# A decoder of two layers on one core: skip diagonals built first, and cross attention's first keys and queries prepared in another order

## The chip, the cores and the metric

The kernel runs on 1 core of one Trainium2 chip. The metric is the device time of one execution in microseconds. Before the change it is 2091.84 us, the median of 3 runs (2086.91 to 2093.14). A part of the program that its engines enter and leave together is called a block here; a barrier of all engines stands between two blocks.

## The reference, cut to what matters

The program computes two decoder layers on x (16 batches, 112 positions, 256 channels) with a context of 16 x 375 x 256. Each sublayer adds to x what it computes from the layer norm of x. The change touches the end of the first sublayer (a selective state space model) and the second (cross attention with 16 heads):

```
for the scan:      y_t = einsum('bdn,bn->bd', h, C_t);  y = y + xc * D;  out = (y * silu(z)) @ W_out + residual
cross attention:   q = x @ Wq + bq;   k, v = split(context @ Wkv + bkv)
                   q = _larope(q, Lq);   k = _larope(k, Lk)
                   scores = einsum('bhqd,bhkd->bhqk', q, k) * 64 ** -0.5
                   attn = softmax(where(context_mask, scores, -inf));   out = (attn @ v) @ Wo + bo
_larope:           re = te * cos - to * sin;   ro = te * sin + to * cos
```

The rest (routed experts, a gated recurrence, an attention by delays, a mixture with soft slots) is the same in both kernels.

## The kernel before

Tokens are columns, channels are partitions. The 1792 tokens are NCH = 4 chunks of CW = 448 columns, each of which holds BPC = 4 batches of L = 112. Every engine has its own instruction list, written out by hand in Python, and semaphores order them. An fp32 matmul of the program shows as two records in the trace.

The scan (`mamba`, lines 811 to 1060). The state space model runs in four passes of STEPS = 16 steps. A step is two scans and a product on VectorE (L988, L992, L997), two products on GpSimd (`feed_y` L932, `read_x` L938), exponentials and scalings on ScalarE (L884, L890, L895), and transposes and sums on TensorE (`feed_x` L1020, `add_up` L1025). Before the first step TensorE turns u (`turn_u`, L1013), VectorE copies it out of PSUM (`move_u`, L965), ScalarE scales it (L895), and TensorE turns the result into x_in (`feed_x(0, 0)`). The term xc * D comes in as a matmul with a diagonal matrix (L1045); VectorE builds its four diagonals (L978) after its four copies, and TensorE waits for them (skip_ready) ahead of `feed_x(0, 0)`.

The projection's block (`project_and_norm`, L1065 to 1152). TensorE projects the four chunks (L1086), VectorE adds them to x (L1120), ScalarE squares (L415), TensorE, ScalarE and VectorE make 1 / standard deviation of every column (L423, L428, L432), TensorE spreads it (L438) and VectorE multiplies (L444). SyncE loads cross attention's weights and the context of batches 0 and 1 in this block (`CrossWeights.load`). GpSimd has no work in it.

Cross attention's block (`cross_attention`). Scores are one bf16 matmul for each head, over 128 rows that hold the products of three bf16 parts of q and k. So q and k are split in three: ScalarE rounds the fp32 value to bf16 (`cast_queries` L1644, `cast_keys` L1606), GpSimd subtracts the rounded part (`lessen_queries` L1363, `lessen_keys` L1359), and ScalarE rounds the rest, until there are three parts. SyncE stores the parts to DRAM (L1309, L1303) and loads them back with a head's channels on the rows of the matmul (`load_queries` L1318, `load_keys` L1329). Before the split, keys and queries are turned (larope): TensorE projects them to PSUM (`keys` L1387, `queries` L1470), VectorE multiplies with cosines and sines out of PSUM (L1506, L1557), and the two halves are summed by GpSimd for keys (L1353, L1354) and by VectorE for queries (L1560, L1561).

At the block's start the order is: the centring of w_o and bo (`centre_columns`, L388 to L392, L1567), then for batches 0 and 1 the keys of that batch and the queries of chunk 0 and chunk 1, then the queries of chunks 2 and 3, then the values of batch 0 (L1398, L1596). SyncE stores and loads in the order keys' parts, queries' parts, keys, queries. Then `batch(b, s)` runs 16 times; in it head h is one turn of a software pipeline: score (L1408), mask and minimum on VectorE (L1518), exponential on ScalarE (L1615), transposes (L1418), copies (L1524, L1621), and the product with v every fourth head (L1433). Keys of batch b + 2 and values of batch b + 1 are made between the heads of batch b. The queries of chunks 2 and 3 are split by ScalarE and GpSimd between the heads of batch 0 at these places:

```
            CAST_QUERIES_AT = (0, 1, 3, 4, 6, 7)
            Q_CASTS = [[1, 2, 3], [4, 5, 6], [7, 9, 11], [8, 10, 12]]
```

## Time and profile before

| | us |
|---|---|
| median of 3 runs | 2091.84 |
| the profiled execution's own time | 2081.57 |
| its span, first to last instruction | 2079.8 |
| scan: its block starts, projection's block starts | 117.7, 469.2 |
| cross attention's block starts (first instruction of GpSimd) | 506.67 |
| first score of batch 0 starts | 542.70 |
| first exponential of batch 0 starts | 544.01 |

| engine | busy us | share of the span |
|---|---|---|
| TensorE | 1794.9 | 86% |
| VectorE | 1483.7 | 71% |
| ScalarE | 1051.8 | 51% |
| GpSimd | 901.1 | 43% |

The shares are over stages with different limits, so they say little of one place. A stage is read in the timeline, where a bracket behind an instruction gives how long its engine had been idle and what ended that.

### The profile page before, as it was taken

Reading aid. Unit: us, or ns where it says so; the run is one execution under the profiler, and the core shown is the slowest. Engines: PE = TensorE matmul, PEld = TensorE weight load, DVE = VectorE, ACT = ScalarE, POOL = GpSimd, SP = SyncE. Lnnn points to the kernel's source line nnn. Section 1 sums busy time; section 2 is a strip of 40 time slices with the busy share of each in tenths; the row PEclk is TensorE's granted clock in tenths of the full one; section 3 lists DMA queues with packets and bytes.
Section 4 is the critical chain, followed back from the end, with each engine's and each line's share of the span. In section 5 each row is a group of like instructions: output and inputs, shape, how many; then the busy total and the mean of one; then the engine's idle time right before and its main releaser. Section 6 shows DMA issues by size and latency. Waiting matters only on the chain. (4 is left out here: it accounts for less than half of the span.)

```text
span 2079.8 us, 32873 instructions
## 1 busy us (share of the span) xinstructions
PE 1794.9 (86%) x11062; PEld 1111.9 (53%) x11062; DVE 1483.7 (71%) x2738; ACT 1051.8 (51%) x2211; POOL 901.1 (43%) x602
## 2 busy tenths in 40 slices
PE   7958877879699999888788889888699989999799
PEld 4334444444476666544344444444564656665699
DVE  6779999994788888669555566555475448787893
ACT  4766666651677878526445455555332131114442
POOL 1269778771522222000466666666100009664342
PEclk9979999999899999999889999999899999999899
DMA  2034434331866566130355455543850044333640
GB/s 70 3 117 133 133 121 141 116 92 63 182 153 163 141 149 145 51 129 1 120 179 179 151 188 166 183 128 78 268 160 1 1 125 143 121 132 128 240 138 17
DMA packets 138157, 257.41 MB, mean 124 GB/s; under 512 B 30662, under 2 KB 94823, under 8 KB 135319
## 3 DMA queue, kind: packets, MB, share of 16 engines
q1 hardware_dynamic: 120358, 212.16, 34.2%
q0 software_dynamic: 13824, 37.77, 6.0%
q10 hardware_dynamic: 3808, 5.38, 1.1%
q8 instruction: 90, 1.47, 0.3%
q14 instruction: 77, 0.62, 0.1%
HBM read 205.82 MB, written 49.44 MB: 123 GB/s over the span
## 5 line engine op out<-in xcount | busy, mean ns | idle before, releaser
L3009 PE MATMUL moe_up_ps<-moe_w_tile,ahead 128*64 128x352 f32 x1152 | 213.7, 518 | 3.1 <-issue 1.1
L2946 POOL DMA_INDIRECT moe_y<-ahead,moe_where x144 | 161.9, 1125 | 120.2 <-DVE ahead L3079 91.1
L2940 POOL DMA_INDIRECT ahead<-moe_tok,moe_where x144 | 143.6, 997 | 147.6 <-POOLq L2517 104.0
L2182 POOL TENSOR_TENSOR soft_power<-soft_logit,soft_high 128x1024 f32<-128x1024 f32 x28 | 66.2, 2366 | 292.8 <-DVE soft_high L2244 292.4
L3153 ACT ACTIVATE moe_w_tile<-moe_w 128x1216 f32 x144 | 175.5, 1220 | 19.7 <-issue 19.7
L1615 ACT ACTIVATE xattn_prob<-xattn_sm,xattn_least 112x375 f32<-112x375 f32 x256 | 154.9, 606 | 55.9 <-DVE xattn_least L1518 51.0
L1518 DVE CUSTOM_DVE_ANT_0 xattn_sm<-xattn_s_ps,xattn_mask 112x375 f32<-112x375 f32 x256 | 137.9, 544 | 51.6 <-PE xattn_s_ps L1408 30.2
L938 POOL TENSOR_TENSOR mamba_x_state<-mamba_x_state,mamba_cx_all 128x896 f32<-128x896 f32 x64 | 133.8, 2090 | 69.1 <-DVE mamba_x_state L988 69.0
L1418 PE MATMUL xattn_pt_ps<-ident,xattn_prob 112*125 112x112 f32 x768 | 131.0, 280 | 20.6 <-ACT xattn_pt L1621 12.4
L1418 PEld LDWEIGHTS xattn_pt_ps<-ident,xattn_prob 112*125 112x125 f32 x768 | 112.3, 189 | 60.6 <-ACT xattn_prob L1615 43.7
L3009 PEld LDWEIGHTS moe_up_ps<-moe_w_tile,ahead 128*64 128x64 f32 x1152 | 85.4, 152 | 102.6 <-issue 93.8
L932 POOL TENSOR_TENSOR xn<-mamba_u,mamba_b_all 128x896 f32<-128x896 f32 x64 | 133.8, 2093 | 13.2 <-DMA mamba_b_all<-mamba_b 13.0
L988 DVE TENSOR_TENSOR_SCAN mamba_x_state<-xn,mamba_x_in 128x896 f32<-128x896 f32 x64 | 128.6, 2010 | 1.9 <-PE mamba_x_in L1020 1.9
L992 DVE TENSOR_TENSOR_SCAN mamba_y_state<-mamba_y_state,xn 128x896 f32<-128x896 f32 x64 | 128.4, 2006 | 0.4 <-ACT mamba_y_state L890 0.4
L3073 DVE TENSOR_TENSOR moe_hid<-ahead,moe_up_ps 128x176 f32<-128x176 f32 x144 | 45.7, 333 | 106.0 <-ACT ahead L3159 67.9
L895 ACT ACTIVATE mamba_scaled<-mamba_w_in,mamba_b_turned 128x256 f32<-128x256 f32 x224 | 96.0, 497 | 44.6 <-PE mamba_x_in L1020 43.6
L1020 PE MATMUL mamba_x_in<-ident,mamba_scaled 128*128 128x128 f32 x448 | 63.3, 283 | 62.7 <-ACT mamba_scaled L895 40.3
L2930 DVE COPY moe_w_tile<-moe_w 128x1216 f32 x144 | 109.6, 803 | 10.0 <-issue 9.8
L1025 PE MATMUL mamba_y<-mamba_x_state,ident 128*128 128x448 f32 x256 | 107.6, 543 | 5.3 <-POOL mamba_x_state L938 5.2
L2273 ACT ACTIVATE soft_power<-soft_power 128x1024 f32<-128x1024 f32 x28 | 29.7, 1059 | 155.5 <-POOL soft_power L2182 155.5
L1025 PE MATMUL mamba_y<-ahead_small,ident 128*128 128x448 f32 x256 | 107.6, 543 | 0.0
L1020 PEld LDWEIGHTS mamba_x_in<-ident,mamba_scaled 128*128 128x128 f32 x448 | 49.7, 144 | 105.4 <-ACT mamba_scaled L895 60.5
(435 smaller groups left out, 4301.2 us busy)
## 6 DMA issues: line engine op xcount, KB each, us to landing
moe_w<-moe_w SPq DMA_DIRECT2D x64, 480.0 KB
soft_w<-soft_w SPq DMA_DIRECT2D x16, 1024.0 KB
mamba_b_all<-mamba_b SPq DMA_DIRECT2D x32, 448.0 KB, 4.6
mamba_cx_all<-mamba_c SPq DMA_DIRECT2D x32, 448.0 KB, 3.9
mamba_cy_all<-mamba_c SPq DMA_DIRECT2D x32, 448.0 KB, 4.6
moe_w_tile<-moe_y SPq DMA_DIRECT2D x14, 1024.0 KB, 7.8
soft_logits<-soft_logit SPq DMA_DIRECT2D x28, 512.0 KB
soft_logit<-soft_logits SPq DMA_DIRECT2D x14, 1024.0 KB, 5.4
```

Source lines behind the costliest of these rows:

```text
L932: pool.tensor_tensor(y_in[:, j % 2], u[:, c0 + j % 2, tok], b_all[:, n % 2], ALU.mult).then_inc(y_fed, 1)
L938: pool.tensor_tensor(x_state[:, j % 2], x_state[:, j % 2], cx_all[:, n % 2], ALU.mult).then_inc(x_read, 1)
L988: dve.tensor_tensor_scan(x_state[:, j % 2], x_decay[:, j % 2], x_in[:, 0:HW], 0.0, ALU.mult, ALU.add).then_inc(x_scanned, 1)
L992: dve.tensor_tensor_scan(y_state[:, 0:HW], y_state[:, 0:HW], y_in[:, j % 2], 0.0, ALU.mult, ALU.add).then_inc(y_scanned, 1)
L1025: mm = pe.matmul(y[:, j % 2, w, 0:CW], g.ident[:], src[:, j % 2, w * CW:(w + 1) * CW], start=False, stop=False, skip_group_check=True)
L1418: mm = pe.transpose(turned_probs(h)[:, c], prob[:, h % RING, c * KC:(c + 1) * KC], g.ident[0:L, 0:L])
L1518: dve.tensor_tensor_reduce(sm[:, h % RING], s_ps[0:L, h % 2, 0:S2], mask[:, s], -SCALE, BIG, ALU.add, ALU.min, least[:, s, head(h):head(h) ...
L1615: act.activation(prob[:, h % RING], sm[:, h % RING], ACT.Exp, bias=least[:, s, head(h):head(h) + 1], scale=-1.0, accum_out=total[:, s, hea ...
L2940: pool.indirect_dma_start(xg[:, 2 * s + i], None, tok_dram, bass.IndirectOffsetOnAxis(ap=where[:, 0, t:t + 1], axis=0)).then_inc(gathered[ ...
L2946: pool.indirect_dma_start(y_dram, bass.IndirectOffsetOnAxis(ap=where[:, 1, t:t + 1], axis=0), y_sb[:, 2 * s + i], None).then_inc(y_stored[ ...
L3009: mm = pe.matmul(up_ps[n * HALF:(n + 1) * HALF, i, 0:2 * I], xT[:, s % 2, at:at + HALF], w_tile[:, s, i, n, h * 2 * I:(h + 1) * 2 * I], st ...
L3153: place_weights = weight_placer(act, 0, lambda to, src: act.activation(to, src, ACT.Copy))
```

## The change

1. In the scan's block VectorE builds the four diagonals ahead of its four copies, and TensorE waits for them after `feed_x(0, 0)`, ahead of the first matmul that reads them.
2. The keys of batch 0 are projected, turned, split, stored and loaded in the projection's block, by a new class FirstKeys: two pairs of matmuls into a PSUM bank that before held every second chunk's spread factors, four products on VectorE, two sums and two subtractions on GpSimd, three casts on ScalarE, three stores and four loads on SyncE. The centring of w_o moves there too. The spread factors of chunks 0, 1 and 2 now share one bank, and chunk 3's go to a bank of the accumulator.
3. In cross attention's block the queries fall in five groups: batch 0 (112 columns), batches 1 to 3 (336 columns), and chunks 1, 2 and 3. Batch 0's are first on TensorE and VectorE; VectorE itself subtracts its parts; one store and its three loads are SyncE's first. Groups 0 and 1 are turned by VectorE as before. Of groups 2 to 4 ScalarE takes the projection out of PSUM with its bias (`keep_queries`, two of 128x448 each), and GpSimd turns them (`turn_queries`, four products and two sums of 128x448 each) while batches 0, 1 and 2 run; their three casts stand at heads 7, 11 and 14 of those batches and their stores behind the keys of batch b + 2. VectorE no longer turns those three chunks.
4. The tensors of the scan that reach into cross attention, and merged, q, q_turn and mask, lie in one tensor ("wide"), so the names in the new program differ. The two loads of the context are no longer next to each other: batch 1's is last in the list.

The diff, cut to its core:

```
         self.own_rows, self.w_kv, self.w_o = view(r, 1494, [NHEAD, D]), view(r, 1750, [P, DH, 2 * D]), view(r, 2774, [P, DH, D])
         self.context, self.keep = view(r, 3286, [P, 2, DH, S2]), view(r, 4786, [L, B * S2 // 4]).bitcast(U8)
         self.small_loaded, self.kv_loaded, self.w_o_loaded = k.kept_sem("xattn_small_loaded"), k.kept_sem("xattn_kv_loaded"), k.kept_sem("xattn_w_o_loaded")
+        self.rope_loaded = k.kept_sem("xattn_rope_loaded")
         self.ctx_loaded = [k.kept_sem(f"xattn_ctx_loaded{s}") for s in range(2)]
...
     def load(self, sp, ins):
         sp.dma_start(self.w_kv, ins["xattn_w_kv"].rearrange("(h p) n -> p h n", p=P)).then_inc(self.kv_loaded, 16)
-        for s in range(2):
-            self.load_context(sp, ins, s, s)
-        sp.dma_start(self.bias, ins["xattn_bias"]).then_inc(self.small_loaded, 16)
-        sp.dma_start(self.rope, ins["xattn_rope"]).then_inc(self.small_loaded, 16)
+        self.load_context(sp, ins, 0, 0)
+        sp.dma_start(self.bias, ins["xattn_bias"]).then_inc(self.rope_loaded, 16)
+        sp.dma_start(self.rope, ins["xattn_rope"]).then_inc(self.rope_loaded, 16)
+        sp.dma_start(self.w_o, ins["xattn_w_o"].rearrange("(c p) n -> p c n", p=P)).then_inc(self.w_o_loaded, 16)
         sp.dma_start(self.w_q, ins["xattn_w_q"].rearrange("(h p) n -> p h n", p=P)).then_inc(self.small_loaded, 16)
-        sp.dma_start(self.w_o, ins["xattn_w_o"].rearrange("(c p) n -> p c n", p=P)).then_inc(self.w_o_loaded, 16)
         sp.dma_start(self.own_rows, ins["xattn_own_rows"]).then_inc(self.small_loaded, 16)
-        sp.dma_start(self.keep, ins["xattn_keep"].partition_broadcast(L)).then_inc(self.kv_loaded, 16)
+        sp.dma_start(self.keep, ins["xattn_keep"].partition_broadcast(L)).then_inc(self.small_loaded, 16)
+        self.load_context(sp, ins, 1, 1)
...
+class FirstKeys:
...
+    def project(self, pe, m, to):
+        c = self.g.cross
+        if m == 0:
+            pe.wait_ge(c.kv_loaded, 16)
+            pe.wait_ge(c.ctx_loaded[0], 16)
+        else:
+            pe.wait_ge(self.half_read, 1)
+        for h in range(DH):
+            mm = pe.matmul(to[:, 0:S2], c.w_kv[:, h, m * P:(m + 1) * P], c.context[:, 0, h], start=(h == 0), stop=(h == DH - 1))
+        mm.then_inc(self.ready, 1)
+
...
+        dve.wait_ge(self.ready, m + 1)
+        cos, sin = c.rope[:, 2 * L:2 * L + S2], c.rope[:, 2 * L + S2:]
+        for n in range(2):
+            product = dve.scalar_tensor_tensor(self.turn[:, 2 * m + n], src[:, 0:S2], c.bias[:, DH + m:DH + m + 1], (cos, sin)[(m + n) % 2], ALU.add, ALU.mult)
+        product.then_inc(self.read if m else self.half_read, 1)
+
+    def centre_out(self, dve):
+        dve.wait_ge(self.g.cross.w_o_loaded, 16)
+        centre_columns(dve, Steps(dve, self.w_o_centred), self.g.cross.w_o, self.w_o_total, self.w_o_mean[:])
+
+    def split(self, act, n):
+        if n == 0:
+            act.wait_ge(self.whole, 1)
+        else:
+            act.wait_ge(self.less, n)
+        act.activation(self.part[:, n], self.key[:], ACT.Copy).then_inc(self.cast, 1)
...
+        pool.wait_ge(self.half_read, 1)
+        pool.wait_ge(self.read, 1)
+        pool.tensor_tensor(key[:, 0], turn[:, 0], turn[:, 2], ALU.subtract)
+        pool.tensor_tensor(key[:, 1], turn[:, 1], turn[:, 3], ALU.add).then_inc(self.whole, 1)
+        for n in range(self.PARTS - 1):
+            pool.wait_ge(self.cast, n + 1)
+            pool.tensor_tensor(key[:], key[:], self.part[:, n], ALU.subtract).then_inc(self.less, 1)
+
+    def move(self, sp):
+        for n in range(self.PARTS):
+            sp.wait_ge(self.cast, n + 1)
+            sp.dma_start(self.dram[0, DH * n:DH * (n + 1)].rearrange("m p t -> p m t"), self.part[:, n]).then_inc(self.stored[n], 16)
+        for first, last, at in sorted(self.K_ROWS, key=lambda rows: rows[1]):
+            sp.wait_ge(self.stored[last - 1], 16)
+            rows = (last - first) * HD
+            sp.dma_start(self.ks[at:at + rows, 0], self.dram[0, DH * first:DH * last].rearrange("n (i h) t -> (n i) h t", h=NHEAD)).then_inc(self.loaded[0], 16)
 
...
-                    for r in range(TURNED):
-                        move_u(0, r)
                     for c in range(DIC):
                         diag = dve.tensor_scalar(skip_diag[:, c], g.ident[:], skip[:, c:c + 1], None, ALU.mult)
                     diag.then_inc(skip_ready, 1)
+                    for r in range(TURNED):
+                        move_u(0, r)
...
-                    pe.wait_ge(skip_ready, 1)
                     for p, (c0, hh) in enumerate(passes):
                         feed_x(p, 0)
+                        if p == 0:
+                            pe.wait_ge(skip_ready, 1)
...
+        places, after = [spread[:, s] for s in range(2)], None
+        if keys:
+
+            places, after = [spread[:, 0]] * 3 + [acc[:, 1, 0]], [0, 1, 2, 0]
+        ln = ChunkNorm(k, ctx, name, g, [var[:, i % 2, 0:L] for i in range(NCH)], places, after)
...
             project(0)
             project(1)
             ln.variance(pe, 0, 0)
+            if keys:
+                keys.project(pe, 0, raw_keys)
             project(2)
             ln.spread_out(pe, 0)
             ln.variance(pe, 1, 0)
+            if keys:
+                keys.project(pe, 1, raw_keys)
             project(3)
             ln.spread_out(pe, 1)
             ln.variance(pe, 2, 1)
@@ -1124,9 +1221,14 @@
             add(0)
             add(1)
             ln.invert(dve, 0)
+            if keys:
+                keys.rotate(dve, 0, raw_keys)
             add(2)
             ln.scale(dve, 0)
             ln.invert(dve, 1)
+            if keys:
+                keys.rotate(dve, 1, raw_keys)
+                keys.centre_out(dve)
             add(3)
             ln.scale(dve, 1)
             ln.invert(dve, 2)
@@ -1142,8 +1244,13 @@
             ln.root(act, 0)
             ln.square(act, 2, added, 3 * DH)
             ln.root(act, 1)
+            if keys:
+                keys.split(act, 0)
+                keys.split(act, 1)
             ln.square(act, 3, added, 4 * DH)
             ln.root(act, 2)
+            if keys:
+                keys.split(act, 2)
             ln.root(act, 3)
...
-            CAST_QUERIES_AT = (0, 1, 3, 4, 6, 7)
+            CAST_QUERIES_AT = (7, 11, 14)
...
+            FIRST, OTHERS = 0, 1
+            GROUPS = [(0, slice(0, L)), (0, slice(L, CW))] + [(j, slice(0, CW)) for j in range(1, NCH)]
+            Q_PLACES = (s_ps, pt_ps, s_ps, pt_ps, s_ps)
...
+                store_queries(FIRST)
+                sp.wait_ge(q_first_stored, 16)
+                load_queries(0, 0)
+                store_parts(1, 1)
+                load_keys(1, 1)
+                store_queries(OTHERS)
+                sp.wait_ge(q_stored[0], 16 * (BPC - 1))
+                load_queries(1, 1)
+                for b in range(B - 2):
+                    if b == 2:
...
+                    pool.tensor_tensor(query(g_no, 1), turned_query(g_no, 1), turned_query(g_no, 3), ALU.add).then_inc(q_whole, 1)
 
                 pool.memset(v[:], 0.0).then_inc(v_cleared, 1)
-                for s in range(2):
-                    sum_keys(s)
-                    for n in range(PARTS - 1):
-                        lessen_keys(s, n)
-                        lessen_queries(s, s, n)
+                sum_keys(1)
+                pool.wait_ge(q_whole, 2)
                 for n in range(PARTS - 1):
-                    for j in range(2, NCH):
-                        lessen_queries(j, j % 2, n)
+                    lessen_keys(1, n)
+                    lessen_queries(OTHERS, n)
                 for b in range(B - 2):
+                    if b < NCH - 1:
+                        turn_queries(OTHERS + 1 + b)
                     sum_keys(b + 2)
                     for n in range(PARTS - 1):
...
+                def keep_queries(g_no):
+
+                    act.wait_ge(q_ready, g_no + 1)
+                    for m in range(DH):
+                        last = act.activation(query(g_no, m), query_ps(g_no, m), ACT.Identity, bias=bq[:, m:m + 1])
+                    last.then_inc(q_kept, 1)
```

In the scan's block, VectorE's list from the end of its clearing to the first scan. Before:

```order
L960 MEMSET xn 128x8 x2
L965 COPY mamba_w_in<-mamba_x_in 128x512 x2
L965 COPY mamba_w_in<-mamba_y_state 128x512
L965 COPY mamba_w_in<-mamba_y_state 128x256
L978 TENSOR_SCALAR ahead_small<-ident,mamba_small 128x128 x4
L988 SCALAR_TENSOR_TENSOR mamba_x_state<-xn,mamba_x_in 128x896
```

With the change:

```order
L1041 MEMSET xn 128x8 x2
L1057 TENSOR_SCALAR ahead_small<-ident,mamba_small 128x128 x4
L1046 COPY wide<-mamba_x_in 128x512 x2
L1046 COPY wide<-mamba_y_state 128x512
L1046 COPY wide<-mamba_y_state 128x256
L1069 SCALAR_TENSOR_TENSOR mamba_x_state<-xn,mamba_x_in 128x896
```

The four diagonals (ahead_small is their place) moved ahead of the four copies; nothing else did.

At the start of cross attention's block, TensorE's list up to the first scores (s_ps, pt_ps and kv_ps are PSUM tensors that queries, keys and values are projected to). Before:

```order
L1476 MATMUL xattn_o_ps<-ahead,mean_w 128x1 x2
L1387 MATMUL xattn_kv_ps<-ahead 128x375 x4
L1470 MATMUL xattn_s_ps<-xn,ahead 128x448 x4
L1387 MATMUL xattn_kv_ps<-ahead 128x375 x4
L1470 MATMUL xattn_pt_ps<-xn,ahead 128x448 x4
L1470 MATMUL xattn_s_ps<-xn,ahead 128x448 x4
L1470 MATMUL xattn_pt_ps<-xn,ahead 128x448 x4
L1398 MATMUL xattn_kv_ps<-ahead 125x256 x6
```

With the change:

```order
L1626 MATMUL xattn_s_ps<-xn,ahead 128x112 x4
L1633 MATMUL xattn_o_ps<-ahead,mean_w 128x1 x2
L1537 MATMUL xattn_kv_ps<-ahead 128x375 x4
L1626 MATMUL xattn_pt_ps<-xn,ahead 128x336 x4
L1626 MATMUL xattn_s_ps<-xn,ahead 128x448 x4
L1548 MATMUL xattn_kv_ps<-ahead 125x256 x4
L1626 MATMUL xattn_pt_ps<-xn,ahead 128x448 x4
L1548 MATMUL xattn_kv_ps<-ahead 125x256 x2
L1626 MATMUL xattn_s_ps<-xn,ahead 128x448 x4
```

One set of key matmuls is gone, batch 0's queries are first, and the values stand between the chunks.

ScalarE's list at the same place, with the change, from the first cast of group 1's queries to the first exponentials (before, six casts of keys and six of queries alternate, then come the copies of the values, the table load and the exponentials):

```order
L1815 ACTIVATE xattn_q_part<-wide 128x2x336
L1756 ACTIVATE xattn_v<-xattn_kv_ps 125x8x16 x4
L1821 ACTIVATE wide<-xattn_pt_ps,ahead 128x448 x2
L1766 ACTIVATE xattn_part<-xattn_key 128x750
L1815 ACTIVATE xattn_q_part<-wide 128x2x336
L122 DMA ahead<-ctxT 128x2x375
L1756 ACTIVATE xattn_v<-xattn_kv_ps 125x8x16 x2
L1821 ACTIVATE wide<-xattn_s_ps,ahead 128x448 x2
L1766 ACTIVATE xattn_part<-xattn_key 128x750
L1815 ACTIVATE xattn_q_part<-wide 128x2x336
L1775 ACT_TABLE_LOAD
L1775 ACTIVATE xattn_prob,xattn_total<-xattn_sm,xattn_least 112x375 x6
```

Behind the last chunk's matmuls there now stand on ScalarE two of `keep_queries`, a cast of keys, a cast of queries and the table load, all ahead of the first exponential.

## Rows read from the trace of the kernel before

**Rows 1.** Timeline, start of the scan's block: start us, us, engine, what [idle, releaser].

```profile
119.95 2.89 ACT L895 ACTIVATE mamba_scaled<-mamba_w_in,mamba_b_turned 128x256 f32<-128x256 f32 x7
...
121.44 4.11 POOL L932 TENSOR_TENSOR xn<-mamba_u,mamba_b_all 128x896 f32<-128x896 f32 x2 [12.95 <-DMA mamba_b_all<-mamba_b]
121.52 4.51 DVE L978 TENSOR_SCALAR ahead_small<-ident,mamba_small 128x128 f32<-128x128 f32 x4
...
126.09 1.76 PE L1020 MATMUL mamba_x_in<-ident,mamba_scaled 128*128 128x128 f32 x7 [5.12 <-DVE ahead_small L978]
...
127.95 2.02 DVE L988 TENSOR_TENSOR_SCAN mamba_x_state<-xn,mamba_x_in 128x896 f32<-128x896 f32 x1 [1.92 <-PE mamba_x_in L1020]
```

**Rows 2.** Windows: us, busy PE, PEld, DVE, ACT, POOL (instructions), granted clock, DMA, GB/s.

```profile
469.20:504.90 35.70, 34.45 (x194) 18.54 (x194) 12.51 (x16) 6.91 (x11) 0.00 (x0) 1.00 0.26 85
506.60:542.70 36.10, 23.25 (x64) 12.99 (x65) 27.49 (x38) 12.87 (x19) 21.04 (x13) 0.81 0.45 103
542.70:563.20 20.50, 18.33 (x146) 12.83 (x146) 15.15 (x47) 16.91 (x43) 10.75 (x7) 0.84 1.02 205
563.20:582.60 19.40, 18.32 (x197) 13.66 (x185) 16.33 (x52) 15.55 (x48) 4.80 (x4) 1.00 0.75 176
```

**Rows 3.** Timeline, from cross attention's block start to its first exponential.

```profile
506.67 2.66 POOL L1365 MEMSET xattn_v<- 125x3072 f32 x1 [42.36 <-POOLq L78]
...
507.30 4.32 PE L1387 MATMUL xattn_kv_ps<-ahead 128*128 128x375 f32 x8
...
514.61 2.69 PE L1387 MATMUL xattn_kv_ps<-ahead 128*128 128x375 f32 x8
...
522.93 2.28 DVE L1560 TENSOR_TENSOR xattn_q<-xattn_q_turn 128x448 f32<-128x448 f32 x1
...
523.14 3.17 PE L1470 MATMUL xattn_pt_ps<-xn,ahead 128*128 128x448 f32 x8
526.15 1.89 PE L1398 MATMUL xattn_kv_ps<-ahead 128*125 128x256 f32 x8
...
540.00 1.28 ACT L1615 ACT_TABLE_LOAD   x1
...
542.70 0.85 PE L1408 MATMUL xattn_s_ps<-xattn_ks,xattn_qs 128*112 128x375 bf16 x2 [3.69 <-DMA xattn_qs<-xattn_q_parts]
...
544.01 0.61 ACT L1615 ACTIVATE xattn_prob<-xattn_sm,xattn_least 112x375 f32<-112x375 f32 x1 [2.73 <-DVE xattn_least L1518]
```

**Rows 4.** Groups by form, 506 to 543 us: busy us, mean ns, idle before.

```profile
L1363 POOL TENSOR_TENSOR xattn_q<-xattn_q,xattn_q_part 128x896 f32<-128x896 f32 x4 | 7.9, 1981 | 2.5 <-ACT xattn_q_part L1644 2.5
...
L1644 ACT ACTIVATE xattn_q_part<-xattn_q 128x896 bf16<-128x896 f32 x6 | 5.7, 949 | 7.8 <-POOL xattn_q L1363 4.7 <-DVE xattn_q L1561 3.1
L1606 ACT ACTIVATE xattn_part<-xattn_key 128x750 bf16<-128x750 f32 x6 | 5.0, 828 | 16.0 <-POOL xattn_key L1354 13.7 <-POOL xattn_key L1359 2.3
...
L1557 DVE SCALAR_TENSOR_TENSOR xattn_q_turn<-xattn_s_ps,ahead 128x448 f32<-128x448 f32 x8 | 4.9, 678 | 2.1 <-PE xattn_s_ps L1470 2.0
```

**Rows 5.** Timeline, two forms that come near to new ones.

```profile
488.06 1.04 PE L438 MATMUL mamba_proj_out_spread<-mamba_proj_out_ln_rstd,pick 128*128 128x112 f32 x8
...
886.76 0.63 ACT L1152 ACTIVATE mean<-xattn_proj_out_acc,xattn_bo_mean 128x448 f32<-128x448 f32 x1 [0.40 <-PE xattn_proj_out_acc L1093]
```

**Rows 6.** DMA issues, 566 to 580 us: count, KB each, median us to landing.

```profile
xattn_qs<-xattn_q_parts SPq DMA_DIRECT2D x2, 168.0 KB, 2.8
```

**Rows 7.** Timeline, batches 0 and 1.

```profile
553.22 3.74 POOL L1363 TENSOR_TENSOR xattn_q<-xattn_q,xattn_q_part 128x896 f32<-128x896 f32 x2 [0.47 <-ACT xattn_q_part L1644]
...
554.07 0.50 DVE L1524 COPY xattn_pt<-xattn_pt_ps 125x336 f32<-125x336 f32 x1
...
563.24 0.35 DVE L1512 TENSOR_SCALAR xattn_mask<-ahead 112x375 f32<-112x375 uint8 x1
...
565.14 0.61 ACT L1615 ACTIVATE xattn_prob<-xattn_sm,xattn_least 112x375 f32<-112x375 f32 x1 [0.47 <-DVE xattn_least L1518]
...
582.60 0.34 DVE L1512 TENSOR_SCALAR xattn_mask<-ahead 112x375 f32<-112x375 uint8 x1
```

307 lines of the change are left out of this document (194 added, 113 removed).

## The prediction

> **What bounds the kernel now.** I read the page's shares first, then the windows of the stages that the change touches [rows 2], then the timeline at three places [rows 1, 3, 5, 7] and the groups for durations [rows 4]. TensorE's 86% says little. In the projection's block it is the bound (34.45 of 35.7 us busy [rows 2]). In the first 36 us of cross attention it is busy for 23.25, at a mean granted clock of 0.81, and no engine is full: that stretch is a chain. It ends with batch 0's first score at 542.70, after TensorE waited 3.69 us for a load of queries, and the first exponential at 544.01 [rows 3]. Before that load stand the keys of batch 0, four query stores, four key loads and three query loads. In the scan VectorE runs one scan after another, so what delays its first delays all: TensorE sat idle 5.12 us until the last diagonal, and the scan began at 127.95 [rows 1].
>
> **1. Diagonals first: -3.2 us.** The diagonals ran from 121.52 for 4.51 us, beside GpSimd's two products (121.44 for 4.11), and `feed_x(0, 0)` began at 126.09. The other thing that it waits for, ScalarE's seven scalings, ends at 119.95 + 2.89 = 122.84 [rows 1]. With the diagonals at about 118, before GpSimd has work, it begins at 122.9, 3.2 us earlier, and the scan with it: 124.8. The copies of u may be later by the diagonals' own time; GpSimd's feeds (done at 125.55) are needed only at the second scan, 2 us later. Bounds: 0, if another input of the first step takes over; -3.3 at most.
>
> **2. Keys in the projection's block: +2.7 us.** TensorE gets four fp32 matmuls of 375 columns there, 2.69 us for that form at full clock [rows 3], and it is the bound [rows 2]. The rest lies beside it: VectorE's four products, the centring of w_o, GpSimd's four operations and ScalarE's three casts (0.83 each [rows 4]) fit in idle time (VectorE 12.51 and ScalarE 6.91 busy of 35.7, GpSimd 0 [rows 2]). What they could hold up is the last add and the last square. If that cover fails, the centring and a cast show: I allow 2.5 us more. SyncE's last key loads must be issued before the block ends; the third cast is about 6 us ahead of the end, a store lands in some 3 us (loads of like size took 2.8 [rows 6]). Bounds: +1.3 (half of the matmuls) and +5.2. The next block then starts at 506.67 - 3.2 + 2.7 = 506.2.
>
> **3. The start of cross attention: -12.2 us to the first exponential.** I add up TensorE from the block's start (506.67 before; its keys begin 0.6 later, behind the sums for bo [rows 3]). Batch 0's queries are eight records of 112 columns: 1.04 us for that form at full clock [rows 5], twice that at half clock, as the trace has it at this start (keys 4.32 us there against 2.69 later [rows 3]). So the keys of batch 1 start at 0.6 + 2.1 = 2.7. Those slow keys ended 5.0 us after the start; I take half of the present ones in that time (2.2) and half after it (1.4): 6.3. Group 1, three quarters of 3.17: 8.7. Chunk 1, 3.17: 11.9. Two thirds of the values, 1.89: 13.8. Chunk 2: 17.0. The last values 1.0: 18.0. Chunk 3: 21.1 [rows 3]. Then ScalarE: two `keep_queries` (0.63 each, by the nearest form [rows 5], overlapping a little) 1.2; only here are the scores let go, at 22.3. A cast of keys 0.83, a cast of three quarters of the queries' 0.95 [rows 4], and the table load of 1.28 [rows 3], which before lay in idle time and now stands in the way: first exponential 25.1 us after the start. Before it was 544.01 - 506.67 = 37.3. Difference -12.2.
>
> I put the DMA path below that. Batch 0's queries are projected by 2.9 and turned by 4.7 (a product of 448 columns takes 0.678 us [rows 4], here a quarter of the columns), cast and lessened in turn with VectorE's key products by about 10, stored (one store instead of four) by 13, and loaded by 17: loads of this kind landed in 2.8 us where the queues were free [rows 6]. So some 5 us of cover lie before 22.3. Batch 1's queries follow its keys and their stores and land at about 38 by the same prices; its first score is due at 22.3 + 21.1 = 43.4 (544.01 to 565.14 [rows 3, 7]). Bounds: -16 (table and last casts hidden, clock full from the start) and -8 (the queries' load last, 4 us late).
>
> **4. Batches 0 to 2: +1.0 us.** From first exponential to the next batch's mask batch 0 took 563.24 - 544.01 = 19.2 us, batch 1 582.60 - 565.14 = 17.5 [rows 7]. Batch 0 had six query casts and a mean clock of 0.84 [rows 2]; so six casts and a slow start cost 1.8 together, a cast at most 0.3. Now each of three batches has three casts: batch 0 loses three casts and the slow start (-0.9), batches 1 and 2 gain three each (+1.7). GpSimd's turning is six operations of 448 columns, about 1.0 us each by half of 1.98 [rows 4], 6 us a batch beside 3.9 of subtractions and 4.8 of keys [rows 2]: 15 of 19.4 us. VectorE's wait for GpSimd is the new cost. `TENSOR_TENSOR` with both inputs in SBUF took 2.28 us while GpSimd worked [rows 3], and the diagonals 4.51 [rows 1], but copies out of PSUM took 0.50 beside it [rows 7]. In a batch only the mask and one reciprocal of VectorE work from SBUF alone; I take +0.2. Here a rule bears. The Trainium skill ("SBUF — State Buffer", section "Who interferes with whom") says that such a pair excludes each other for a whole instruction, while a VectorE instruction with at most one SBUF input outside its two-port modes does not contend. By it the price is at most two waits of one GpSimd operation for each batch, and the rows above agree. Bounds: -2 and +5.
>
> **Sum:** -3.2 + 2.7 - 12.2 + 1.0 = -11.7 us. Against the profiled execution's own 2081.57 us (span 2079.8) that is 2069.9. The median of the runs shown is 2091.84, 0.5% above that execution; the same difference on it gives **2080.1 us**. A measurement of this kernel can tell about 0.3% (6.3 us) from no change.
>
> **The rivals.**
> - *The chain at the start gets shorter still.* TensorE keeps its full clock and ScalarE's last casts slip in before the keeps: part 3 gives -16 and batch 0 runs at batch 1's pace with its casts. Gain 3.2 - 2.7 + 16 + 0 = 16.5: 2075. For it: of those 25 us, 2.8 are casts and table load and more than 4 are at half clock. Against it: ScalarE's list is in order and the table load is behind the last cast.
> - *ScalarE becomes the bound of batches 1 and 2.* It is busy 15.55 of 19.4 us in batch 1 [rows 2]; three casts of 0.95 make 18.4. If every cast shows, part 4 is 6 x 0.95 - 0.9 + 0.2 = +5.0: gain 7.7, 2084.1. Against it: six casts in batch 0 cost 1.8 at most.
> - *The diagonals do nothing.* If another input of the first step (a load of b or c, a decay) comes as late, 3.2 is missing: 2083.3. Against it: the rows show none after 125.6.
> - *Slower: GpSimd keeps VectorE out.* If every operation of VectorE in batches 0 to 2, not only those from SBUF alone, waited for GpSimd, the added GpSimd work would go on top: 9.9 us in each, less batch 0's four subtractions of 1.98 [rows 4] that are gone, 22 in all. -3.2 + 2.7 - 12.2 + 22 = +9.3, 2101.1. It decides from about 13 us of such waits. For it: 2.28 us for a sum of 448 columns while GpSimd worked [rows 3]. Against it: 0.50 for the copy in the middle of GpSimd's work [rows 7].
>
> **How the numbers follow.** Forecast 0.62, shorter chain 0.12, ScalarE 0.14, diagonals 0.07, slower 0.05. The range reaches from the shorter chain's 2075 less 2 for the runs' own spread to the ScalarE case's 2084.1 with part 2 at its upper bound (+2.5) and the same spread: 2073 to 2089. Faster by over 0.3% means below 2085.6: the forecast nearly always (0.59), the first rival (0.12), the others that remain in half their cases (0.10): 0.81. Within 0.3%: 0.14. Slower: 0.05.
>
> **What the profile would show.** Right: first scan at about 124.8 with TensorE's wait for ScalarE, not the diagonals; cross attention's block starts at about 506.2; first score at about 528.5 with no DMA as releaser but ScalarE's keep; first exponential at about 531.3 behind a table load; mask to mask in batches 1 and 2 under 20.5 us. Wrong: the first score waiting for a load of queries or of keys; the projection's block longer by over 5 us, or ended by SyncE; batch 1's first score waiting for its queries; VectorE's operations out of PSUM longer than 0.5 us in batches 0 to 2.

## The result and the profile after

| | before | after |
|---|---|---|
| median of 18 runs, us | 2095.26 | 2083.31 |
| lowest and highest, us | 2086.91, 2099.80 | 2075.81, 2095.41 |
| span of the profiled execution, us | 2079.8 | 2074.0 |

The ratio is 0.9939, 95% interval 0.9928 to 0.995: 12.8 us less by the ratio, 10.5 to 15.1 by its interval. The forecast was 11.7 us less and 2080.1, with a range of 2073 to 2089.

First the scan, by the timeline (start us, us, engine, line, operation, in brackets the idle time before it and what ended that). It answers to [rows 1].

```profile
115.23 0.29 DVE L1057 TENSOR_SCALAR ahead_small<-ident,mamba_small 128x128 f32<-128x128 f32 x1
115.43 0.67 DVE L1057 TENSOR_SCALAR ahead_small<-ident,mamba_small 128x128 f32<-128x128 f32 x3
117.34 2.88 ACT L976 ACTIVATE mamba_scaled<-wide,mamba_b_turned 128x256 f32<-128x256 f32 x7
...
120.28 1.76 PE L1101 MATMUL mamba_x_in<-ident,mamba_scaled 128*128 128x128 f32 x7 [1.92 <-ACT mamba_scaled L976]
...
122.14 2.02 DVE L1069 TENSOR_TENSOR_SCAN mamba_x_state<-xn,mamba_x_in 128x896 f32<-128x896 f32 x1 [3.15 <-PE mamba_x_in L1101]
```

The four diagonals take under 1 us, where beside GpSimd they took 4.51, and TensorE now waits for ScalarE's scalings, as forecast. The block starts at 115.10 (117.72 before; what lies ahead is the same program, so these 2.6 us are the execution's own). From the block's start the scan begins after 7.04 us instead of 10.23.

Next the start of cross attention, against [rows 3]. The block starts at 503.18, and the distances behind the rows are from there.

```profile
503.18 2.66 POOL L1514 MEMSET xattn_v<- 125x3072 f32 x1 [8.95 <-POOLq L78]
503.37 2.02 PE L1626 MATMUL xattn_s_ps<-xn,ahead 128*128 128x112 f32 x8 [3.25 <-PEq L78]
...
505.93 4.48 PE L1537 MATMUL xattn_kv_ps<-ahead 128*128 128x375 f32 x8
...
510.24 2.42 PE L1626 MATMUL xattn_pt_ps<-xn,ahead 128*128 128x336 f32 x8
...
512.50 3.17 PE L1626 MATMUL xattn_s_ps<-xn,ahead 128*128 128x448 f32 x8
...
514.72 1.23 SPq L1452 DMA_DIRECT2D xattn_qs<-xattn_q_parts  x3
514.73 0.51 DVE L1715 TENSOR_TENSOR wide<-wide 128x336 f32<-128x336 f32 x1
...
521.11 3.17 PE L1626 MATMUL xattn_s_ps<-xn,ahead 128*128 128x448 f32 x8
...
524.31 1.16 ACT L1821 ACTIVATE wide<-xattn_s_ps,ahead 128x448 f32<-128x448 f32 x2 [1.01 <-PE xattn_s_ps L1626]
...
525.52 0.53 PE L1558 MATMUL xattn_s_ps<-xattn_ks,xattn_qs 128*112 128x375 bf16 x2 [1.25 <-ACT wide L1821]
...
526.86 1.28 ACT L1775 ACT_TABLE_LOAD   x1
...
528.15 0.61 ACT L1775 ACTIVATE xattn_prob<-xattn_sm,xattn_least 112x375 f32<-112x375 f32 x1
```

From the block's start, batch 1's keys begin after 2.75 us, group 1 after 7.06, chunk 1 after 9.32, the last chunk ends at 21.1, the first score runs at 22.34, released by ScalarE's keep (the copy of the last chunk's queries out of PSUM) and not by a load, and the first exponential at 24.97, right behind the table load. Before, it was 37.34. Batch 0's queries are loaded by 11.5 + 1.2 (three issues) + 2.9 (the median landing of such loads here) = 15.7, by estimate.

The windows (us, busy PE, PEld, DVE, ACT, POOL with counts, granted clock, DMA share, GB/s) of the projection's block, of the start, and of batches 0 to 3, which answer to [rows 2].

```profile
463.10:503.20 40.10, 36.98 (x202) 20.05 (x202) 16.85 (x23) 9.40 (x14) 4.79 (x5) 0.99 0.47 127
503.20:525.50 22.30, 20.90 (x64) 13.21 (x64) 7.84 (x21) 8.41 (x20) 10.51 (x8) 0.86 0.25 66
525.50:545.70 20.20, 17.39 (x146) 12.28 (x146) 14.88 (x47) 15.72 (x41) 11.51 (x10) 0.92 0.67 136
545.70:566.40 20.70, 18.62 (x194) 13.74 (x186) 16.26 (x52) 17.73 (x52) 15.10 (x12) 1.00 0.84 177
566.40:587.30 20.90, 18.38 (x190) 13.60 (x186) 16.31 (x52) 18.01 (x54) 15.11 (x12) 1.00 0.82 177
587.30:608.10 20.80, 18.29 (x189) 13.60 (x185) 16.38 (x53) 17.32 (x52) 6.62 (x5) 1.00 0.84 178
```

The projection's block is 40.1 us long instead of 37.5 (469.2 to 506.67). Its last cast of keys and the loads of them:

```profile
494.26 0.83 ACT L186 ACTIVATE xattn_part<-xattn_key 128x750 bf16<-128x750 f32 x1
495.52 3.74 SPq L205 DMA_DIRECT2D xattn_ks<-xattn_k_parts  x4
```

In the start TensorE is busy for 20.9 of 22.3 us. ScalarE is busy for 17.3 to 18.0 of 20.8 us in batches 1 to 3. From mask to mask these batches take 20.7, 20.9 and 20.7 us, where before they took 19.4, 20.1 and 20.1.

Where the sum of the two traces then goes is the surprise. At the last exponential the changed kernel is 14.7 us ahead (844.8 against 859.5), at the first product of the routed experts 17.2 (988.0 against 1005.2). The experts' stage, where the change does nothing, took 463.4 us instead of 450.6, and the end is 5.8 us ahead. Yet the medians say 12. The kernel before was profiled in an execution of 2081.57 us, below all of its 18 runs (the lowest is 2086.91); the changed one in its fastest (2075.81). So the two traces understate the change. The first question for the runs was still whether the change slows the experts.

### The profile page after: what moved, and what is told of

Same layout as the page of the kernel before. It is cut to its first block and busy times, and to the rows that moved or that the text cites. A ratio compares the mean times of both kernels' runs of the same rounds, so it can differ in the third digit from the quotient of the medians.

```text
span 2074.0 us, 32902 instructions
## 1 busy us (share of the span) xinstructions
PE 1790.3 (86%) x11070; PEld 1111.4 (54%) x11070; DVE 1463.1 (71%) x2728; ACT 1053.7 (51%) x2220; POOL 917.2 (44%) x620
## 5 line engine op out<-in xcount | busy, mean ns | idle before, releaser
L1676 DVE CUSTOM_DVE_ANT_0 xattn_sm<-xattn_s_ps,wide 112x375 f32<-112x375 f32 x256 | 137.6, 542 | 54.0 <-PE xattn_s_ps L1558 26.3
L1013 POOL TENSOR_TENSOR xn<-mamba_u,mamba_b_all 128x896 f32<-128x896 f32 x64 | 133.9, 2095 | 14.9 <-DMA mamba_b_all<-mamba_b 14.7
L3115 DVE COPY moe_w_tile<-moe_w 128x1216 f32 x144 | 109.2, 799 | 11.3 <-issue 11.0
L976 ACT ACTIVATE mamba_scaled<-wide,mamba_b_turned 128x256 f32<-128x256 f32 x224 | 95.8, 495 | 40.2 <-PE mamba_x_in L1101 39.2
L1682 DVE COPY xattn_pt<-xattn_pt_ps 125x336 f32<-125x336 f32 x192 | 96.5, 503 | 16.2 <-PE xattn_pt_ps L1568 15.7
```

The lines of the kernel that those rows point to most:

```text
L1013: pool.tensor_tensor(y_in[:, j % 2], u[:, c0 + j % 2, tok], b_all[:, n % 2], ALU.mult).then_inc(y_fed, 1)
L1676: dve.tensor_tensor_reduce(sm[:, h % RING], s_ps[0:L, h % 2, 0:S2], mask[:, s], -SCALE, BIG, ALU.add, ALU.min, least[:, s, head(h):head(h) ...
```

## The experiments

In every kernel below, each copy that places an expert's weights waits against the expert's number masked with 63 (one register operation more, in the experts' stage); `before_again` shows that it costs nothing visible (a ratio of 0.9999). Kernels of one group ran on one chip, and the three groups on three chips; for the first pair the record names no chip. A mask (the row of VectorE that makes one batch's mask) marks the same point of each batch; times from mask to mask are read from the timelines, and batch 1 runs from mask 1 to mask 2.

**The pair again, and the diagonals alone and undone.**

> The kernel before, with one register operation more at each of the copies that place an expert's weights (the number that the copy waits for is masked with 63); the base of the others. Theory: within 0.2% of the kernel before, stages as in its trace, and a routed-experts stage (first to last product of moe_up) that differs between profiles of one kernel by some +-6 us, near 455 in the mean. Rival (the change itself slows the experts by the 12.8 us that the two traces differ by): this kernel has 450 to 452 again, after_again 462 to 465.

> The changed kernel, with the same mask. Theory: 11 to 14 us less than before_again in the medians; experts' stage within 5 us of before_again's in the second pair of profiles, so that the 12.8 us of the first pair are the runs' own spread. Rival: the experts' stage is 10 us or more longer again, and then the difference up to the experts must be 22 us or more.

> before_again with the diagonals ahead of the copies of u and nothing else of the change. Theory: first scan 3.2 us earlier after its block's start (7.0 instead of 10.2), released by ScalarE's scalings; total -3 us. Rival (another input or a later wait of the scan takes it back): first scan earlier but the projection's block starts at the same distance from the scan's block as in before_again, total 0 within 1 us.

```diff
-                    for r in range(TURNED):
-                        move_u(0, r)
                     for c in range(DIC):
...
                     diag.then_inc(skip_ready, 1)
+                    for r in range(TURNED):
+                        move_u(0, r)
...
-                    pe.wait_ge(skip_ready, 1)
                     for p, (c0, hh) in enumerate(passes):
                         feed_x(p, 0)
+                        if p == 0:
+                            pe.wait_ge(skip_ready, 1)
```

> after_again with the diagonals back behind the copies of u. Theory: +3.2 us against after_again, first scan 10.2 us after its block's start; cross attention as in after_again, so the rest of the change alone is worth 9 us. Rival (parts depend on each other or the diagonals are hidden): no difference within 1 us.

Its edit is the same one backwards. Measured on one chip, the kernel before at 2022.45 us (35 runs):

| kernel | median us | ratio to before | interval | scan begins | experts' stage |
|---|---|---|---|---|---|
| before_again | 2022.43 | 0.9999 | 0.998 to 1.0017 | 125.9 | 391.3 |
| before_diag | 2021.65 | 0.9995 | 0.9975 to 1.0016 | 122.6 | 390.7 |
| after_nodiag | 2012.75 | 0.9956 | 0.9935 to 0.9977 | 125.9 | 392.9 |
| after_again | 2012.02 | 0.9949 | 0.9931 to 0.9968 | 122.2 | 394.1 |

The change is worth 10.3 us here (6.5 to 14.0 by the interval), a little under the 11 to 14 expected. The experts' stage does not lengthen by 12.8 us again; it is 2.8 longer in this pair and 2.2 in the other, so the rival (10 us or more) is gone, though 2 to 3 us are not excluded. On this chip the stage is 60 us shorter than the 455 us that I expected, in all four kernels; the last section takes that up. The diagonals' move is plain in the rows, `before_diag` first, `before_again` behind it:

```profile
120.71 1.76 PE L1020 MATMUL mamba_x_in<-ident,mamba_scaled 128*128 128x128 f32 x7 [1.92 <-ACT mamba_scaled L895]
122.57 2.02 DVE L988 TENSOR_TENSOR_SCAN mamba_x_state<-xn,mamba_x_in 128x896 f32<-128x896 f32 x1 [3.15 <-PE mamba_x_in L1020]
```

```profile
119.47 4.54 DVE L978 TENSOR_SCALAR ahead_small<-ident,mamba_small 128x128 f32<-128x128 f32 x4
124.06 1.75 PE L1020 MATMUL mamba_x_in<-ident,mamba_scaled 128*128 128x128 f32 x7 [5.15 <-DVE ahead_small L978]
125.92 2.02 DVE L988 TENSOR_TENSOR_SCAN mamba_x_state<-xn,mamba_x_in 128x896 f32<-128x896 f32 x1 [1.92 <-PE mamba_x_in L1020]
```

From ScalarE's scalings (117.77 and 117.90) the scan begins 4.80 us later instead of 8.02, so it gains 3.2; in the other pair it is 4.80 and 8.01. Counted from the start of the scan's block, the projection's block begins 3.7 us earlier (348.4 against 352.1), and 3.9 in the other pair (348.2 against 352.1), so no later wait of the scan takes it back. But the totals differ by 0.8 and 0.7 us where 3 were expected, and each has an interval of some 4 us to either side. A gain of 3 us is shown at its place, and neither shown nor refuted in the time.

**The start made shorter, in three steps.** The kernel before: 2080.84 us (27 runs).

> after_again with one exponential of a single element put on ScalarE before the last keeps of queries, so that the exponentials' table is loaded there, where ScalarE waits for TensorE. Theory (the start is a chain of TensorE's list and then ScalarE's list in its order): the load of 1.28 us goes off the path, first exponential 1.3 us earlier after the block's start (23.7 instead of 25.0), first score unchanged at 22.3. Rival (the batch 0 loads or the first score's bias set it): under 0.3 us. Total -1 us, less than the medians can tell.

```diff
                 copy_values(0, 0, 2)
+                act.activation(recip[0:1, 0:1], g.ident[0:1, 0:1], ACT.Exp)
                 keep_queries(4)
```

> table, and the last cast of batch 1's keys and of its queries put behind the first three exponentials. Theory: the first exponential then waits only for the first score, its bias of 0.55 us and the table: score 22.3 + 0.2 + 0.6 = 23.1 after the block's start; the 1.5 us of casts come back behind it only in part, batch 1's keys and queries being ready with 5 us to spare. Rival (batch 1's loads become late): TensorE waits for a load at batch 1's first score and the mask-to-mask time of batch 0 rises by over 1 us.

```diff
-                cast_keys(1, 2)
-                cast_queries(OTHERS, 2)
                 for h in range(3):
                     exponentiate(0, 0, h)
+                cast_keys(1, 2)
+                cast_queries(OTHERS, 2)
```

> table_casts, and the first three scores put ahead of the last chunk's queries on TensorE, those queries written where the sums of the first batches come (free until the first weigh), with their keeps on ScalarE behind the first exponentials. Theory: batch 0's queries and keys are in place by 17 us after the block's start, so the first score runs at about 18.2 (after the last values) and the first exponential at about 19.2, 5.8 us earlier than in after_again; the 3.2 us of queries and 1.2 us of keeps then stand in batch 0, where TensorE is near its bound, so that mask 1 comes only 2 to 4 us earlier. Total -2 to -4 us against after_again. Rival (the path of batch 0's queries over DMA is the real bound and has no cover): the first score waits for a load of queries or keys, and the gain at the first exponential is under 2 us.

```diff
-            Q_PLACES = (s_ps, pt_ps, s_ps, pt_ps, s_ps)
+            Q_PLACES = (s_ps, pt_ps, s_ps, pt_ps, o_ps)
...
+                pe.wait_ge(q_kept, 1)
+                for h in range(3):
+                    scores(0, 0, h)
                 queries(4)
-                pe.wait_ge(q_kept, 3)
-                for h in range(4):
-                    scores(0, 0, h)
+                scores(0, 0, 3)
+                pe.wait_ge(q_kept, 2)
                 for h in range(2):
                     turn_probs(0, 0, h)
+                pe.wait_ge(q_kept, 3)
...
+                for h in range(3):
+                    exponentiate(0, 0, h)
                 keep_queries(4)
-                for h in range(3):
-                    exponentiate(0, 0, h)
                 cast_keys(1, 2)
```

Distances from the block's start in us:

| kernel | ratio to before (interval) | first score | first exponential | mask 1 | batch 1 | batch 2 | batch 3 |
|---|---|---|---|---|---|---|---|
| before, first trace | | 36.0 | 37.3 | 56.6 | 19.4 | 20.1 | 20.1 |
| after, first trace | 0.9939 (0.9928 to 0.995) | 22.3 | 25.0 | 42.5 | 20.7 | 20.9 | 20.7 |
| table | 0.996 (0.9935 to 0.9985) | 22.7 | 23.9 | 40.0 | 20.7 | 20.9 | 22.4 |
| table_casts | 0.9967 (0.9952 to 0.9981) | 22.6 | 23.7 | 40.6 | 23.7 | 22.5 | 20.7 |
| early_scores | 0.9967 (0.9955 to 0.9979) | 17.9 | 21.5 | 39.4 | 24.6 | 20.9 | 22.4 |

`table` gains 1.0 us at the first exponential, not 1.3, since the table load and its one-element exponential held the last keep up by 0.5 us (it starts at 526.09, TensorE's last chunk ends at 525.64). But at mask 1 it gains 2.5, and the rest has another cause. Windows of the changed kernel, then of `table`, around and behind the first exponential (the last three numbers are the granted clock, DMA share, GB/s):

```profile
526.00:529.00 3.00, 0.88 (x4) 0.35 (x3) 1.58 (x6) 2.97 (x6) 3.00 (x4) 1.00 0.65 144
529.00:532.00 3.00, 2.99 (x12) 2.14 (x13) 2.27 (x7) 2.27 (x8) 2.90 (x3) 0.64 0.99 188
532.00:535.00 3.00, 3.00 (x14) 2.18 (x13) 1.44 (x4) 1.20 (x5) 0.00 (x0) 0.79 1.02 240
```

```profile
526.00:529.00 3.00, 0.99 (x4) 0.41 (x4) 1.04 (x5) 3.00 (x7) 3.00 (x4) 1.00 0.03 10
529.00:532.00 3.00, 2.99 (x17) 2.03 (x18) 2.70 (x9) 2.27 (x9) 2.92 (x3) 1.00 1.03 225
532.00:535.00 3.00, 3.00 (x38) 2.12 (x37) 2.65 (x9) 2.23 (x7) 1.36 (x2) 1.00 0.99 196
```

In the changed kernel TensorE has only four scores to do between 524.3 and 528.9, and behind that stretch its clock is at 0.64 and 0.79 of 2.4 GHz, a mix of the two levels; in 529 to 535 it gets 26 matmuls of its list through. In `table` the stretch is 3.6 us (525.6 to 529.2), the clock stays at 1.00, and 55 of the same list get through. All seven profiles with the table load in its old place show the lower clock there (0.60 to 0.68 and 0.76 to 0.83 in the two windows of 3 us behind the stretch), and the three with only the table load and casts moved (`table`, `table_casts`, `best`) show 1.00. That the clock makes all of the other 1.5 us is not measured by itself.

`table_casts` and `early_scores` show the other wall. In `early_scores` the first score runs at 17.9 with no wait for a load, so batch 0's loads have at least the 4.4 us of cover down to 22.3. Its first exponential was expected at 19.2 and came at 21.5: the table load stands behind two casts and a copy of values on ScalarE, and the exponential comes right behind it. Its rows of the first score, of the table load, and of batch 1's first score:

```profile
522.43 0.48 PE L1558 MATMUL xattn_s_ps<-xattn_ks,xattn_qs 128*112 128x375 bf16 x2
524.64 1.28 ACT L1855 ACT_TABLE_LOAD   x1
546.56 0.34 PE L1558 MATMUL xattn_s_ps<-xattn_ks,xattn_qs 128*112 128x375 bf16 x1 [1.86 <-issue]
```

Batch 1 has less cover. The loads of its queries and its first score, in `table_casts`:

```profile
545.42 2.65 SPq L1452 DMA_DIRECT2D xattn_qs<-xattn_q_parts  x6
...
549.68 0.53 PE L1558 MATMUL xattn_s_ps<-xattn_ks,xattn_qs 128*112 128x375 bf16 x1 [2.24 <-issue]
```

In the changed kernel, by the timeline of SyncE's queue and of TensorE:

```profile
530.56 1.90 SPq L1443 DMA_DIRECT2D xattn_q_parts<-xattn_q_part  x3
539.42 6.53 SPq L1452 DMA_DIRECT2D xattn_qs<-xattn_q_parts  x6
...
546.36 0.32 PE L1558 MATMUL xattn_s_ps<-xattn_ks,xattn_qs 128*112 128x375 bf16 x1
```

There they are in by 539.42 + 1.2 (three issues) + 2.9 = 543.5, by estimate, 2.8 us ahead of use. From the last issue of the stores ahead of them (532.46) to the first load it is 7.0 us, and batch 1's key loads stand in front of these stores; that they are the cause was not separated. Two casts behind three exponentials moved the first load from 36.2 to 39.3 us after the block's start, and TensorE waited 2.24 us, with the clock at 0.50 for the 3 us behind it. The profile names no releaser ("issue"), but the same estimate puts the queries in at 545.42 + 1.2 + 2.9 = 549.5, and the score starts at 549.68. What `early_scores` won at the start it paid in batch 1, 24.6 us. So the rival named for `table_casts` came true (batch 1's loads are late; the time shows in batch 1, not in batch 0). The one named for `early_scores` did not: batch 0's path has cover, and it is batch 1's that has none to spare. (The single batches of 22.4 and 22.5 us are taken up in the last section.)

None of the three ratios (0.996 to 0.9967) is better than the changed kernel's (0.9939, and 0.9949 on another chip), and those of `table_casts` and `early_scores` have intervals above its first one. The changed kernel did not run on this chip, so this is no direct comparison. The rows agree with it: `table_casts` gains 2.0 us to mask 1 and loses 4.6 in batches 1 to 3, `early_scores` gains 3.1 and loses 5.5; `table` gains 2.5 and loses 1.6, all of it in batch 3.

**What lengthens batches 1 to 3.** The next kernel was executed once, on the same chip.

> after_again without ScalarE's nine casts of queries in batches 0 to 2 (what is stored for batches 4 to 15 is then the parts of the first chunk; the output leaves the other chunks' queries out). It tells what lengthens batches 1 to 3 by 0.7 to 1.4 us against before. If it is ScalarE: mask to mask in batches 1, 2 back to 19.4 to 20.1. If it is GpSimd's turning (VectorE kept out, or keys late): 20.7 and 20.9 stay, within 0.2.

```diff
-                        if b < NCH - 1 and h in CAST_QUERIES_AT:
-                            cast_queries(OTHERS + 1 + b, CAST_QUERIES_AT.index(h))
```

Beside these lines, the stores and GpSimd's subtractions of these groups no longer wait for a cast; GpSimd does the same work, 15.1 us in each of batches 1 and 2.

Batches 1 to 3 took 20.3, 19.9 and 19.6 us, 2.6 in sum less than in the changed kernel, and batch 0 did not move (mask 1 at 42.5). So in sum ScalarE's casts, with what waits for them, make 2.6 of the 2.8 us by which these batches had grown, and GpSimd's turning next to nothing (the three batches take 59.8 us without the casts, and 59.5 to 59.8 in the three profiles with the old cross attention). Batch by batch it is less clean: the casts cost 0.45, 1.06 and 1.1 us, and batch 1 stays 0.9 us above the 19.4 of the kernel before, while batches 2 and 3 are 0.3 and 0.4 below its 20.1. The cause of that stays open. Batch 3 has only one cast, the one at head 14 of batch 2, and it cost 1.1 us. The trace shows how: it stands ahead of ScalarE's copy of turned probabilities, and TensorE waits for that copy. Three such waits stand in the changed kernel's timeline, and in the same batches TensorE has no wait over 1 us in `no_casts`, in `before` or in `casts_moved` below:

```profile
550.92 0.55 PE L1568 MATMUL xattn_pt_ps<-ident,xattn_prob 112*125 112x112 f32 x3 [1.45 <-ACT xattn_pt L1781]
571.81 0.55 PE L1568 MATMUL xattn_pt_ps<-ident,xattn_prob 112*125 112x112 f32 x3 [1.44 <-ACT xattn_pt L1781]
592.73 0.55 PE L1568 MATMUL xattn_pt_ps<-ident,xattn_prob 112*125 112x112 f32 x3 [1.44 <-ACT xattn_pt L1781]
```

**The casts moved, the best start, and GpSimd's work doubled.** The kernel before: 2093.49 us (11 runs).

> after_again once more, on the chip of the next three: their base. Theory: 0.5 to 0.6% under the kernel before; mask-to-mask times of the first batches as in both traces of it (20.7, 20.9, 20.7) and a granted clock below 1.00 for some 6 us behind the first exponential.

> after_third with ScalarE's first cast of each group of queries at head 5 instead of 7, and its last at head 4 of the next batch instead of head 14. In the trace ScalarE runs without a gap from head 7 of a batch to head 2 of the next, and idles before heads 1 to 6. Theory (a cast costs its full 0.9 us where ScalarE has no gap, nothing where it has): mask to mask 20.2 in batch 1, 19.9 in batch 2, 19.7 in batch 3, 2 us less in all. Rival (the casts cost by what they trigger: GpSimd's subtractions beside VectorE): the three stay above 20.6.

```diff
-            CAST_QUERIES_AT = (7, 11, 14)
+            CAST_QUERIES_AT = (5, 11)
...
+                        if 0 < b < NCH and h == 4:
+                            cast_queries(OTHERS + b, 2)
```

> casts_moved, with the exponentials' table loaded by a one-element exponential at the very start of ScalarE's list, where it is idle for 5 us. Theory: first score 22.3 and first exponential 23.6 us after the block's start (25.0 in after_third); the stretch in which TensorE does little shortens from 4.6 us to 3.2 and its clock stays at 1.00 behind it, worth 1.5 us more; with the casts, 5 us less than after_third. Rival (the compiler puts a second table load where it was): no difference from casts_moved.

```diff
+                act.activation(recip[0:1, 0:1], g.ident[0:1, 0:1], ACT.Exp)
                 for n in range(PARTS):
                     cast_first(n)
```

> after_third with GpSimd's four products of each turned group done twice (the same result; 4.4 us more of GpSimd in each of batches 0 to 2). Theory: GpSimd has gaps of 3.4 us and more before the keys' sums, VectorE's operations read at most one operand from SBUF: up to 1 us more per batch, by keys that become whole later. Rival (GpSimd keeps VectorE out, the slower case of the prediction): 4.4 us more per batch, the copies out of PSUM longer than 0.5 us.

```diff
+                    for time in range(2):
-                    for n, table in enumerate((q_cos, q_sin, q_sin, q_cos)):
+                        for n, table in enumerate((q_cos, q_sin, q_sin, q_cos)):
...
+                        pool.wait_ge(q_turned, 2 * (g_no - OTHERS) - 1 + time)
```

| kernel | ratio to before (interval) | first exponential | mask 1 | batch 1 | batch 2 | batch 3 |
|---|---|---|---|---|---|---|
| after_third | 0.9946 (0.9925 to 0.9968) | 24.8 | 42.4 | 20.7 | 20.9 | 20.7 |
| casts_moved | 0.9939 (0.992 to 0.9959) | 24.9 | 42.5 | 20.6 | 20.7 | 20.1 |
| best | 0.994 (0.992 to 0.9959) | 23.4 | 39.5 | 20.4 | 20.7 | 20.1 |
| turn_twice | one run | 25.0 | 42.5 | 20.7 | 20.9 | 20.7 |

`casts_moved` gained half of the 2 us expected: the three waits are gone, but batches 1 and 2 hardly move, so the heads to which the casts went are not free. `best` gains 2.8 us to mask 1, with the clock at 1.00 behind the first exponential (0.60 and 0.83 in `after_third`), and 1.2 us in batches 1 to 3: 4.1 us by the rows, 5 expected. Its median of 2081.18 against 2081.90 of `after_third`, with intervals of some 4 us, doesn't show it. So `best` is faster than the kernel before, by the intervals; whether it is faster than the changed kernel stays open.

`turn_twice` put 4.3 to 4.4 us more of GpSimd into each of batches 0 to 2 (19.5 us of 20.7 in batch 1) and moved no batch by over 0.05 us against the changed kernel. Its row of VectorE's copies out of PSUM, then that of the changed kernel (528 to 590 us; busy us, mean ns, idle before):

```profile
L1683 DVE COPY xattn_pt<-xattn_pt_ps 125x336 f32<-125x336 f32 x36 | 18.2, 504 | 5.2 <-PE xattn_pt_ps L1569 5.1
```

```profile
L1682 DVE COPY xattn_pt<-xattn_pt_ps 125x336 f32<-125x336 f32 x36 | 18.1, 502 | 5.2 <-PE xattn_pt_ps L1568 5.1
```

The products fitted into GpSimd's waits for the keys, and no copy out of PSUM grew.

**The experts' stage over all profiles.** From the first to the last product of `moe_up`, windows of the kernel before, the changed kernel (first traces), `after_third` and `after_again`:

```profile
1005.20:1455.80 450.60, 395.99 (x2818) 197.72 (x2820) 261.37 (x649) 237.30 (x426) 292.57 (x276) 0.93 0.51 157
```

```profile
988.00:1451.40 463.40, 400.27 (x2820) 200.23 (x2822) 260.36 (x649) 237.80 (x426) 291.85 (x276) 0.92 0.50 152
```

```profile
991.40:1462.50 471.10, 407.87 (x2820) 201.86 (x2822) 259.44 (x649) 239.84 (x426) 293.42 (x276) 0.91 0.50 150
```

```profile
991.00:1385.10 394.10, 368.68 (x2820) 190.79 (x2822) 262.76 (x649) 239.16 (x426) 293.79 (x276) 0.98 0.59 179
```

It took 391 to 394 us in four profiles of the first group, 452 to 460 in four of the second, 464 to 471 in four of the third. Within a group the kernels differ by up to 8 us where their code is the same, and the first pair, by 12.8, may not even be of one chip. So one pair of profiles can't show a difference of 12 us in the total. The batches from mask 4 to the last exponential, the same code too, took 236.7 to 242.2 us in the four profiles of the first group.

## Why the prediction was right, by its own steps

1. **Diagonals, forecast -3.2:** -3.19 by the first traces, -3.2 in both pairs on one chip, with the releaser named. That it reaches the end is not shown by the totals.
2. **Keys in the projection's block, +2.7:** +2.6. TensorE was the bound, as forecast (36.98 of 40.1 us busy). The centring and the casts lay beside TensorE's work. The last cast ended at 495.1, 6.3 us ahead of VectorE's last operation in the block (which ends at 501.35), where I had 6.
3. **The start, -12.2:** 37.34 to 24.97 is -12.4. The list of TensorE was right at its end (21.1) though not inside: the keys ended at 7.1 instead of 6.3, since the clock was at 0.50 until some 6 us after the start instead of 5, and the next four groups each made up some 0.2 us by overlapping, which I had not counted. The table load stood in the path. `early_scores` shows at least 4.4 us of batch 0's cover, where I had about 5. Batch 1's was mis-sized: its queries are in at 40.3 and used at 43.2, where I had 38 and 43.4, because the stores took 7 us behind the keys where I took some 3. In the changed kernel that cost nothing.
4. **Batches 0 to 2, +1.0:** +1.15, by errors that cancel. To mask 1 batch 0 took 17.56 us, 1.7 less than before where I had 0.9 less; batches 1 and 2 took 1.4 and 0.8 more, where I had 0.85 each; and batch 3, which I had left out, 0.7 more. One sign that I had named as right failed: batches 1 and 2 from mask to mask under 20.5 us took 20.7 and 20.9. The step was right that casts cost about 0.3 each on average (nine make 2.6), but gave them an even price: the two of batch 0 at heads 7 and 11 are free, and the one that batch 3 has, at head 14, costs 1.1, by what stands behind it in ScalarE's list. That the total came out at +1.15 is luck. The 0.2 for GpSimd was not needed.

Sum: -3.2 + 2.6 - 12.4 + 1.15 = -11.8, against a measured gain of 12.8 by the first ratio and 10.3 and 11.3 by the two repeats. The forecast of 2080.1 stood on a median of 2091.84 of three runs; over 18 it was 2095.26, which makes the 3.2 us between forecast and result. The ratios can't tell 11.8 from 10 or 13, so it is the rows that confirm parts 1 to 3.

The rivals: the shorter chain (2075) did not happen. Even `best`, made for it, brings the first exponential 1.4 us forward where this rival needs 3.8. ScalarE as bound was right in its place and wrong in its size: 2.6 us, not 5.0. The diagonals did act. GpSimd does not keep VectorE out: the forecast's slower case needed 13 us of such waits, and `turn_twice` has none. By the Trainium skill ("SBUF — State Buffer", section "Who interferes with whom") VectorE's operations with at most one operand from SBUF, outside its two-port modes, don't contend, and the copies out of PSUM agree (502 and 504 ns). The same section counts `tensor_scalar` among the operations that can enter such a mode. That bears on what reads only SBUF: the four diagonals took 4.51 us beside GpSimd and 0.96 without it, and the mask, 0.34 us in the changed kernel, took 0.90 in `no_casts`, where it ended 0.2 us behind a subtraction of GpSimd. Which mode they were in no run shows.

```profile
546.44 1.89 POOL L1504 TENSOR_TENSOR wide<-wide,xattn_q_part 128x896 f32<-128x896 f32 x1
547.65 0.90 DVE L1672 TENSOR_SCALAR wide<-ahead 112x375 f32<-112x375 uint8 x1
```

On the table load the Trainium skill ("ScalarE: Activation LUTs", section "What ACT_TABLE_LOAD costs") gives 1.28 us for the load and about as much again for a drain. The trace has the 1.28 but no drain: the cast ends at 526.84, the load starts at 526.86 and the exponential at 528.15. The forecast counted the row alone, and with the drain it would have been some 1.5 us too late.

## What to carry to other kernels

Add up the start of a stage along the list of the engine that fills it, and then along the engine behind it, table load included; that sum held within 0.2 us here, with errors of up to 0.8 us inside it. When an operation is moved into a full engine, ask what stands right behind it and who waits for that, not how busy the engine is: one cast of 0.95 us cost 1.1 us at head 14 (in batch 3) and nothing at two heads of batch 0. A gain of 3 us in 2080 is seen in the rows of its stage, not in the total, and a pair of profiles must be compared stage by stage, since an untouched stage can differ by more than the change is worth.
